# Three bfloat16 parts in place of one float32 matmul for the decay sums of a gated delta rule layer

## The reference, cut to what matters

```python
g = -jnp.exp(A_log) * jax.nn.softplus(x @ Wa.T + dt_bias)      # (B, L, H), log decay of a token and head
g_full = zeros(B, L, NH, H).at[:, :, 0].set(g)                 # the first of a token's two steps decays
def step(state, inp):
    q_t, k_t, v_t, g_t, b_t = inp
    state = state * jnp.exp(g_t)[..., None, None]
    corr = jnp.einsum('bhk,bhkv->bhv', k_t, state)
    state = state + jnp.einsum('bhk,bhv->bhkv', k_t, (v_t - corr) * b_t[..., None])
    return state, jnp.einsum('bhk,bhkv->bhv', q_t, state)
```

## Time and profile before

| | us |
|---|---|
| median of 3 runs | 598.84 (597.14 to 604.26) |
| the profiled execution | 599.72 |
| its span, first to last instruction | 597.9 |
| PE busy in the span | 552.3 |
| DVE busy | 458.7 |
| ACT busy | 365.6 |
| POOL busy | 40.7 |

### The profile page before, as it was taken

How to read it: one execution, slowest core, us unless ns; L and a number is a source line. 1 busy time by engine, 2 the same in 40 slices (tenths; PEclk the granted TensorE clock), 3 DMA queues, 4 the chain that set the end, 5 groups by cost and what they waited for, 6 DMA issues and landing times.

```text
span 597.9 us, 15569 instructions
## 1 busy us (share of the span) xinstructions
PE 552.3 (92%) x6516; PEld 375.6 (63%) x6516; DVE 458.7 (77%) x1087; ACT 365.6 (61%) x651; POOL 40.7 (7%) x74
## 2 busy tenths in 40 slices
PE   8798889999999999999999999999998699767997
PEld 5446347576657666766676667667756688555646
DVE  5778888797888878887888788878794624799663
ACT  2785775694669466946685668566854145477351
POOL 6341000100010001000100100010000000100000
PEclk9989999999999999999999999999998699977999
DMA  6001111102110200021002101210022400000002
GB/s 167 2 7 43 23 37 50 25 10 39 42 23 11 70 11 22 14 67 12 21 15 67 12 20 17 65 21 11 2 44 47 137 8 3 9 1 1 1 0 71
DMA packets 49702, 18.65 MB, mean 31 GB/s; under 512 B 39100, under 2 KB 48352, under 8 KB 49632
## 3 DMA queue, kind: packets, MB, share of 16 engines
q1 hardware_dynamic: 49632, 17.66, 12.3%
HBM read 14.49 MB, written 3.15 MB: 29 GB/s over the span
## 4 chain that ended last, share of the span: by engine, by line
PE 73%; DVE 10%; ACT 9%; issue 3%; SPq 2%; DMA 1%; POOL 0%; DVEq 0%; ACTq 0%
PE bank L1439 17%; PE bank L1488 7%; DVE acc L979 5%; PE bank L1611 4%; PE bank L1607 4%; PE bank L1797 4%; PE bank L1491 3%; PE bank L1385 3%; PE bank L1569 3%; PE bank L1623 3%; PE bank L1617 2%; PE bank L1485 2%; PE bank L1619 2%; PE bank L1621 2%; PE bank L1859 2%
## 5 line engine op out<-in xcount | busy, mean ns | idle before, releaser
L979 DVE SCALAR_TENSOR_TENSOR acc<-bank,cw,acc 128x508 f32<-128x508 f32 (+2 forms) x240 | 176.5, 739 | 42.7 <-ACT acc L621 38.2
L1439 PE MATMUL bank<-xnT,wq 128*128 128x512 f32 x320 | 154.7, 610 | 12.4 <-DVE acc L979 11.5
L1439 PEld LDWEIGHTS bank<-xnT,wq 128*128 128x128 f32 x320 | 56.6, 191 | 72.1 <-issue 45.2
L621 ACT ACTIVATE acc<-bank,cw 128x512 f32<-128x512 f32 x80 | 55.4, 693 | 49.6 <-PE bank L1439 40.6
L1488 PE MATMUL bank<-kq 128*128 128x384 f32 x128 | 50.9, 497 | 0.0
L1012 DVE SCALAR_TENSOR_TENSOR AM<-bank,rb,DT 128x384 f32<-128x384 f32 x64 | 38.1, 607 | 1.8 <-PE bank L1488 1.5
L563 POOL TENSOR_TENSOR Yc<-T 128x256 f32<-128x256 f32 x7 | 4.3, 613 | 399.7 <-PE bank L1584 399.7
L638 ACT ACTIVATE vT<-acc 128x512 f32<-128x512 f32 x16 | 10.9, 679 | 33.3 <-DVE acc L979 33.2
L1078 DVE SCALAR_TENSOR_TENSOR xres<-bank,f,xres 128x256 f32<-128x256 f32 x56 | 23.7, 476 | 8.5 <-PE bank L1611 8.3
L1037 DVE TENSOR_TENSOR tmp<-Yl,Bl 128x15 f32<-128x15 f32 (+7 forms) x120 | 24.2, 201 | 6.9 <-DMA Bl<-blocks 4.8
L1491 PEld LDWEIGHTS bank<-kq 128*128 128x128 f32 x128 | 22.1, 190 | 10.4 <-issue 3.1
(11 more groups left out here) (323 smaller groups left out, 1134.7 us busy)
## 6 DMA issues: line engine op xcount, KB each, us to landing
wq<-in_w_qkv SPq DMA_DIRECT2D x8, 640.0 KB, 4.1
blocks<-AM SPq DMA_DIRECT2D x128, 8.0 KB, 1.5
xres<-in_x SPq DMA_DIRECT2D x2, 512.0 KB, 4.5
Yl<-in_y_init SPq DMA_DIRECT2D x8, 128.0 KB, 2.6
Bl<-blocks SPq DMA_DIRECT2D x8, 128.0 KB, 2.0
wg<-in_w_gate SPq DMA_DIRECT2D x8, 128.0 KB, 2.1
solved<-Yl SPq DMA_DIRECT2D x8, 128.0 KB, 1.7
Yc<-solved SPq DMA_DIRECT2D x64, 16.0 KB, 2.0
```

The lines of the kernel that those rows point to most:

```text
L621: a(acc[:, u % RING, :, :], bank[6 + u % 2][:, :].rearrange("p (b l) -> p b l", b=4), ACT.Copy, scale=cw[:, t, 3:4]).then_inc(s_tap.next(f ...
L979: stt(w, ps[:, :, 0:L - s], cw[:, t, 3 - s:4 - s], w, ALU.mult, ALU.add).then_inc(s_cv.next(f"u{u}_{s}"), 1)
L1439: ins = mm(bank[6 + u % 2][:, :], wq[:, cc, t, :], xnT[:, cc, 512 * half:512 * half + 512], start=cc == 0, stop=cc == KC - 1)
```

## The change

The log decays are split into three bfloat16 parts (`gl3`): the rounded value, the rounded remainder, and what remains of that. POOL does it once, with five 64-column operations behind `gl`. `decay_rows` multiplies each part with the triangle of ones into a bfloat16 `Gb` of three parts, by halves of the batches: six tensor_tensor operations of 512 columns, with a semaphore increment behind the third and the sixth, where one operation of 1024 columns stood. Every float32 matmul with `seg` becomes three bfloat16 matmuls with `pastb` or `pastbw`, accumulated in the same bank. DVE makes `pastb` in its `gates()` with one cast more. In two of the PE lists dt0 and dt1 move: in the plain list dt0 goes behind mt', and dt1 behind projection 4 and my', to just ahead of dt2; in FIRST dt1 goes behind projection 9. NEXT keeps its order. The two constants `seg` and `bsig` move into memory of `W1`, which is first written in stage 1.

```diff
@@ the lists of PE @@
-TENSOR_ORDER = ("0 1 ly' 2 3 dt0 mt' dt1 4 my' dt2 w1_0' w1_1' r2_0' 5 r2_1' 6 w2_0' w2_1' o0' o1' 7 sa' rs' ca "
+TENSOR_ORDER = ("0 1 ly' 2 3 mt' dt0 4 my' dt1 dt2 w1_0' w1_1' r2_0' 5 r2_1' 6 w2_0' w2_1' o0' o1' 7 sa' rs' ca "
...
-FIRST_TENSOR_ORDER = ("0 1 2 3 4 5 6 7 8 dt0 dt1 9 dt2 ca cs nrm e1_0 e1_1 e2_0 e1_2 e1_3 e2_1 e1_4 e1_5 e2_2 e1_6 e1_7 "
+FIRST_TENSOR_ORDER = ("0 1 2 3 4 5 6 7 8 dt0 9 dt1 dt2 ca cs nrm e1_0 e1_1 e2_0 e1_2 e1_3 e2_1 e1_4 e1_5 e2_2 e1_6 e1_7 "
...
-        Gb = sb("Gb", [P, B, L])
+        Gb = sb("Gb", [P, 3, B, L], BF16)
+        gl3 = sb("gl3", [P, 3, B, H], BF16)
...
-        seg = sb("seg", [P, 2, P])
-        segw = sb("segw", [P, 2, P])
+        pastb = sb("pastb", [P, 2, P], BF16)
+        pastbw = sb("pastbw", [P, 2, P], BF16)
...
-        bsig = sb("bsig", [P, CH, 2, H])
...
+        seg = W1[:, 4:6, :]
+        bsig = W1[:, 6:8, :].rearrange("p k (c n h) -> p (k c) n h", n=2, h=H)
...
-        s_gb = Signal(sem("decay_rows_ready"), ["gb"])
+        s_gb = Signal(sem("decay_rows_ready"), ["0", "1"])
...
-                g.tensor_copy(segw[:, :, here], seg[:, :, there])
+                g.tensor_copy(pastbw[:, :, here], seg[:, :, there])
...
             pool.wait_ge(s_preG.sem, s_preG.at("gl"))
+            pk(g.tensor_copy(gl3[:, 0, :, :], gl[:, :, :]))
+            pk(gt(r2, gl[:, :, :], gl3[:, 0, :, :], ALU.subtract))
+            pk(g.tensor_copy(gl3[:, 1, :, :], r2))
+            pk(gt(r2, r2, gl3[:, 1, :, :], ALU.subtract))
+            pk(g.tensor_copy(gl3[:, 2, :, :], r2))
...
-                g.tensor_tensor(Gb[:, :, :], rep(lower.rearrange("p (o l) -> p o l", o=1), 1, B), rep(gl[:, :, hs], 2, L), ALU.mult).then_inc(s_gb.next("gb"), 1)
+                for f in range(2):
+                    bs = slice(4 * f, 4 * f + 4)
+                    for part in range(3):
+                        i = g.tensor_tensor(Gb[:, part, bs, :], rep(lower.rearrange("p (o l) -> p o l", o=1), 1, 4), rep(gl3[:, part, bs, hs], 2, L), ALU.mult)
+                    i.then_inc(s_gb.next(str(f)), 1)
...
                 v.tensor_copy(segb[:, :, :], cst[:, 4:6, :])
+                v.tensor_copy(pastb[:, :, :], seg)
...
-                if name == "dt0":
-
-                    pe.wait_ge(s_gb.sem, s_gb.at("gb", h))
+                if name in ("dt0", "dt1"):
+
+                    pe.wait_ge(s_gb.sem, s_gb.at(name[2], h))
...
-                        mm(o[:, bs], (seg, segw)[f][:, 1, :], Gb[:, bs, 64:L], start=True, stop=False)
+                        for part in range(3):
+                            mm(o[:, bs], (pastb, pastbw)[f][:, 1, :], Gb[:, part, bs, 64:L], start=part == 0, stop=False)
...
-                    mm(o, (seg, segw)[i][:, 0, :], Gb[:, 4 * i:4 * i + 4, :], start=True, stop=False)
+                    for part in range(3):
+                        mm(o, (pastb, pastbw)[i][:, 0, :], Gb[:, part, 4 * i:4 * i + 4, :], start=part == 0, stop=False)
```

2 lines of the change are left out of this document (1 added, 1 removed).

## The result

| | before | after |
|---|---|---|
| median of 20 runs | 598.77 (596.17 to 604.81) | 606.13 (597.50 to 617.04) |
| the profiled execution | 599.72 | 597.5 |
| its span | 597.9 | 595.7 |
| its mean granted clock | 0.974 | 0.974 |

A forecast was written before the change was run, and what follows sets the result against it. PE was taken as the bound, busy 552.3 of 597.9 us. Terms of -0.3 (stage -1), -1.0 (stages 1 to 5) and +0.4 (stage 6) gave -0.9, rounded to -1.3: 597.5 us from median 598.84, range 594 to 602.

The forecast's parts named there:

- PE's gain: dt tiles on PE: dt0 and dt1 each fall by 0.20 us, dt2 by 0.15 to 0.32; 0.6 to 0.7 a head.
- the walk: Stage 2 on PE in the new order: dt0 and dt1 0.98 us each, dt2 0.87 to 1.04; 0.1 left at w1_0'.
- The two waits: Stage 2 on PE: waits of 0.35 us ahead of mt' and 0.15 ahead of projection 4, taking 0.5 of the saving.
- Stages 1 to 5: Full stages: 0.2 us saved in each, between 0 and 0.7, so -1.0 over five.
- POOL: Decay rows: six 512-column operations, one every 1.0 us, halves 3.05 and 6.05 behind the start, hidden in stage 2.
- The rival of late rows: POOL operations over 1.53 us delay dt1 in every stage, up to 20 us, 619 us; chance 0.04 (milder form 0.16).
- Stage 6: PE waits 0.9 us ahead of dt1 for POOL's second half; stage +0.4 us, from -0.5 to +6.
- The prologue: POOL's extra work for head 0 and `beta` stays hidden; ACT loses a 0.29 wait at projection 9: -0.3 us.
- Stage 0: ACT loads a table before dt0's exponentials and PE is not the bound, so nothing is won: 0 us.
- the one on stage 7 and the epilogue: Stage 7 and the epilogue: 0 us, since nothing changed there.
- the clock: Rival: shifted idle time adds or removes a stretch at 1.2 GHz, 2 us either way; chance 0.15.

The follow-up runs named there:

- rows_early: Changed kernel, but POOL makes the rows of head h+2 right behind dt2 of head h+1, half a stage earlier: 631.92 us, ratio 1.0438.
- before_64: Kernel before, three of its 44 idle start matmuls written as 35 tiny ones, 64 instructions later: 611.24 us against 601.49.
- padded: Changed kernel, eight of its 44 idle start matmuls written as 104 tiny ones, 256 instructions over before: 599.6 us, ratio 0.9985; repeated 600.32 us, 0.9982.
- after_320: Changed kernel, its idle start written as 33 idle and 139 tiny matmuls, 64 + 256 instructions over before: 609.52 us, ratio 1.0131.
- before_256: Kernel before, 11 of its 44 idle start matmuls written as 139 tiny ones, 256 instructions later: 602.79 us, ratio 1.0035.

## Why the prediction was wrong, point by point

**Its steps, one by one.** The first five came as forecast or nearly so, the last two did not.
- *PE's gain*: 0.87 for dt1, where the walk had 0.98 (the 0.11 that it kept for a tile behind small ones did not come back), and 0.88 for dt2, at the good end of 0.87 to 1.04. The three parts hold PE 0.22 each. The Trainium skill's 131 ns for N=512 (TensorE: Matmul & The Clock Gate, Back-to-back issue gap) is not what this trace shows.
- *The two waits*: mt' at 172.08, 0.35 behind the end of projection 3 (171.30 + 0.43), as forecast. The other was forecast at projection 4 with 0.15, and is there with 0.24: dt0 took 0.11 less than the walk gave it, and projection 4 starts 2.68 behind the end of projection 3, as forecast.
- *Stages 1 to 5*: 0.2 us each was the forecast, 0.28 each was measured over four.
- *POOL*: 1.05 an operation and one every 1.0, as forecast. The rival of late rows never came near.
- *Stage 6*: a wait of 0.9 at dt1 was forecast, about 0.6 came, mostly since POOL's rows began at 399.89 and not at 400.24. From the w1_0' of stage 5 to that of stage 6 it is 56.04 us, before 55.79: 0.25 later, where 0.4 was forecast.
- *The prologue*: the norms' result on DVE stood at 47.40 in place of 47.84, 0.4 earlier, where 0.3 was forecast. The next operation, rb, took it back:

```profile
47.97 1.04 DVE L1007 TENSOR_TENSOR rb<-ri,beta 128x16 f32<-128x16 f32 x1
...
43.90 6.08 POOL L560 TENSOR_TENSOR Gb<-cst,gl 128x512 bf16<-128x512 f32 x6 [0.97 <-PE bank L1495]
```

against 0.19 in the earlier trace rows. POOL's `beta` was done at 42.94, so it is no wait for that. It is what rows_early showed: rb reads two tensors from SBUF, and POOL is in the middle of head 1's rows, whose fifth operation ends at 48.98; rb ends at 49.01. In all 13 profiles where rb starts within an operation of POOL it takes 0.69 to 1.06 and ends 0.03 to 0.05 behind that operation; in the seven others, where POOL is done by then, it takes 0.19. It costs the first stage 0.85, once. The prediction walked POOL through the rows of head 0 and `beta` and left out that those of head 1 come in stage -1 too, now for 6.08 us in place of 1.92.
- *Stage 0*: 0 was forecast, 0.9 was lost, of it 0.6 in two waits put down to issue. One of the two in the list of waits between 84 and 105 us, in which before has none of PE (the other is 0.2, L1397):

```profile
PE bank L1583 <- issue: 0.4, 1, 0.4
```

The prediction's terms give -0.9. The profiled execution of after lies 2.2 below that of before, 1.1 of it in stages 1 to 4; it loses 1.1 ahead of them, and gains 2.3 between the w1_0' of stage 6 and that of stage 7, where before has a gap by issue of 1.52 us (up to 452.39) and after none over 0.3. So the 2.2 is in part the place of the gaps and not the work of the change: it is no confirmation of the -0.9.

**The step that failed** is the one on stage 7 and the epilogue: "0 in stage 7 and the epilogue, where nothing changed". The code there is the same, but 64 instructions more stand in front of it, and that changes where in the work PE comes to the end of a piece. before_64 shows that this alone can cost 10 us, and padded shows that with it undone the change gives 0.9985 and 0.9982 of before, -0.9 and -1.1 us, which agrees with the forecast of -1.3, though no change at all lies within both intervals too.

**The term that was mis-sized** is the clock. The prediction had it as a rival, "a shift of idle time by tenths can add or remove such a piece: 2 us either way", with a chance of 0.15. The row it was read from, 0.97 in stage 6, does not show how much such a piece can cost where PE has no idle time to absorb it: in after_320 stage 7, with 10.2 us at half the clock, is 5.3 us longer, and the stretches ahead of and behind it are at a lower clock too (behind it 0.91, where before has 0.93). It should have stood at 5 to 10 us on the bad side. The chance was too small as well, since the change did not shift idle time by tenths at random, but moved every piece of code behind the first stage.

**Shown and not shown.** Shown by runs: the loss follows PE's instruction count, with the bfloat16 sums (after, after_320 against padded) and without them (before_64 against before, before_256), and counts that differ by a whole 256 behave alike in both; neither order nor POOL makes it. Shown by profiles: the gaps stand multiples of 256 instructions apart, each 1.2 to 1.6 us behind the landing of a packet of code. PE out of code is the one reading that fits both. Argued: that such a gap is what lowers the clock. In stage 7 seven of the ten profiles with a gap of over 1.2 us go to half the clock in it or up to 2.1 behind it, and none of the other ten, with 0.81 at most, does. In all stages ahead of the epilogue it is 18 of 23 gaps of over 1.2 us, and 3 of the 109 shorter ones. Before has one itself, 1.52 us up to 452.39 in stage 6, and it is behind this gap that the clock falls for the 0.97 of the earlier trace rows. No run lengthened a gap by itself, so this stays a strong coincidence. Open: why some executions of the changed kernel have the same gap and keep their clock, as the recorded one does, what lowers the clock ahead of stage 1 in before_64 and before_256 alike, and why 224 is better than 0 by 3 to 4 us.

## What to carry to other kernels

Count the instructions that an edit adds ahead of a stretch of tiny matmuls, not only its work, and look in the page of before for idle time put down to issue: a saving of 1 us can turn into a loss of 8 by where the pieces of code end. When the local steps come true and the median does not, compare the granted clock of all runs before looking for a lost wait, and test with idle instructions at the start, which add no work to the stages. A kernel that is tuned by the time of its runs is tuned to one such place, so a new version deserves to be tried at several.

## What the runs showed of the hardware that I had not expected

- 64 idle instructions more at the start of the program, 35 matmuls of 32x32 for three of 256 columns, cost 10 us of 600 (611.2 against 601.5). The changed kernel with 160 more of them, 224 over before, takes 595.5 where it took 606.1 as it was (not beside each other; the runs of before beside them had 599.2 and 598.8).
- All 132 idle times of PE of over 0.3 us by issue ahead of the epilogue stand at instruction 193 or 194 modulo 256 of its count, in 20 profiles, and end 1.2 to 1.6 us behind the landing of a packet of code.
- At the end of one gap of 1.54 us began 10.2 us at 1.2 GHz (after_320), and the last 230 matmuls of the stage took 14.8 us. In before_256, with gaps of up to 0.40, the clock was at 1.00 over the last 230, which took 11.6.
- A DVE operation with both inputs in SBUF that meets a POOL tensor_tensor of 512 columns is held until that one ends, 0.95 to 0.98 us in place of 0.20 (rows_early) and 1.04 in place of 0.19 (rb in after), and POOL keeps its time (6.08 for six). One that reads a bank keeps its 0.74 beside it.
- POOL's tensor_tensor takes as long with bfloat16 operand and result as a float32 one by its size, 1.05 us for 512 columns.
